# Small TensorE products spaced in the planner by instruction packets, and beta moved to one side of the delta rule

## The chip, the cores and the metric

The kernel runs on one core of one Trainium2 chip. The metric is the device time of one execution in microseconds (us). Three runs of the kernel before took 5138.00, 5150.58 and 5158.77 us; the median, 5150.58 us, is the time that counts.

## What is computed

There are 16 sequences of 512 tokens with 256 channels and 16 heads of 16 channels. Every one of them goes through three parts, of which only the first is touched.

```
q, k, v = x @ Wq + bq, x @ Wk + bk, x @ Wv + bv          # per head, 16 channels
k = k / (norm(k) + 1e-6);  beta = sigmoid(x @ Wbeta + bbeta)
S = S + beta_t * outer(v_t - S k_t, k_t);  o_t = S q_t      # the delta rule, one token after another
first = outputs @ Wo + bo                                    # gated delta net
second = causal attention over 16 heads, with RMS norm and rotary positions
third  = mixture of 16 experts, top 4, and a shared expert
```

Each of the blocks (delta net with experts, then attention with experts) is normalised before and added to its input.

## The kernel before, in words

The whole program is one list of stages, written by `stages()` (line 150 on). Each engine walks through the same list in its own function (`tensor`, `vector`, `scalar`, `gpsimd`, `sync`) and issues its own instructions of each stage, with semaphore waits between engines. So the list sets each engine's order of work, and an engine never goes past an instruction that waits. No stage is reordered at run time.

**The first stretch, delta net.** The tokens of one head are worked on in chunks of 16 tokens. One step of the list, m = 0 to 63, takes 128 rows: one chunk of each of 8 sequences; state is kept over the 32 steps of each half. For one m the stages are: `p_qk`, `p_v` (TensorE projections), `p_qk_out`, `p_v_out` (ScalarE copies, squares of k, and tanh for beta), `k_sum` (VectorE, L1387, sum of squares of 16 channels), `k_pow` (GpSimd, L1926 to L1944), `k_scale` and `k_turn` (VectorE, L1388 to L1409), `k_split` (ScalarE copies of k; on GpSimd L1950, which writes `keo`, keys parted by even and odd chunks), `d_pairs` (TensorE, L1073, products of the keys with keys and queries, two halves), `d_keep`, `d_send` and `d_fetch` (through HBM, so that the 16x16 triangles lie along the free axis), `d_row` (VectorE, 15 rows of forward substitution for two m at once, L1426 and L1429), `d_back` and `d_inverse` (through HBM again, L2055 and L2065), and then the recurrence: `s_read` (TensorE, L1087), `s_rest` (VectorE), `s_solve` (TensorE, L1098), `s_took` (ScalarE), `s_add` (TensorE, L1112), `s_new` (VectorE), and `d_out` (TensorE, L1123) with `s_rows`. Buffers of kqT, vT, k01, pairs and inv are a ring of NR = 7, so `p_qk` of m comes after `d_out` of m - 7; qk, vs, ks, beta and pw have two.

Before the change both v and k carry sqrt(beta): `k_pow` makes 1 + tanh (L1931), takes the square roots of the norm and of that number in one power of 32 elements (L1936), adds 1e-6 and multiplies by sqrt(0.5) (L1938, L1939), and scales v (L1942).

**Products of 32x32.** `d_pairs`, `s_read`, `s_solve`, `s_add` and `d_out` consist of 32x32 products in the four row and column strips of TensorE. In the trace each such product is two weight loads and two matmuls: 256 instructions for one `s_read`, `s_solve`, `s_add` or `d_out`, and 128 for one half of `d_pairs`.

**The planner.** Generators (strands) yield stages, and `turn_of` (L176) picks the next strand. `put` keeps a clock for each engine from the table TAKES (us for each stage and engine) and notes when a stage would be done; a strand may go on when TensorE's clock has reached its time `at`. The recurrence (`chain`) comes first in the list of strands, then `rows` (d_out), `relate` (d_pairs), `scale`, `project`, `solve`, `fetch`, `normalise` and `lift`, and behind these the experts' work: `heads`, `shares`, `sums` (gathers of expert output, y_ stages) and `tiles` (t_ stages). A rule holds `rows` and `relate` back for one turn if the latest TensorE stage was one of the five of FINE:

```
if latest[0] in FINE:
    able = [t for t in able if t not in fine] or able
```

`x_move` scatters rows to the experts by indirect DMAs of GpSimd (L2000), and `y_gather` fetches the experts' rows (L2009). A group of expert tiles can begin only after the rows of its four sequences are all scattered. The second stretch (attention, from about 2480 us) has a fixed order with a credit for tiles, and behind it the last tiles are worked off.

## Time and profile before

| what | value |
|---|---|
| median of 3 runs | 5150.58 us |
| the profiled execution, its own time | 5180.71 us |
| span of that profile | 5179.1 us |
| TensorE matmul busy | 3770.6 us (73%) |
| VectorE, ScalarE, GpSimd busy | 2499.1, 1987.3, 2069.6 us (48%, 38%, 40%) |
| mean granted clock of TensorE | 0.821 |
| instructions | 149179 |

The profile is one execution. The share of busy time is an average over stretches with different limits: the delta net takes the span up to about 2480 us, the attention up to about 4860 us, and the tail of expert tiles the rest. "issue" behind an idle time is time in which the engine waited for nothing that the profile shows.

### The profile page before, as it was taken

The page shows a single profiled execution, that of the slowest core. Times are in us where ns is not written, and L with a number is a line of the kernel's source. Part 1 is how long each engine was busy: PE and PEld are TensorE (multiplying, and loading weights), DVE is VectorE, ACT ScalarE, POOL GpSimd, SP SyncE. Part 2 cuts the span into 40 slices and gives each one's busy share as a digit, 9 for nine tenths or more (in the row PEclk, how much of TensorE's full clock was granted, in tenths as well). Part 3 has the DMA queues.
Part 4 walks back from the last instruction along what each step waited for, and adds up shares of the span by engine and source line. Part 5 has one row for each costly group of instructions (what it writes and reads, how often), then busy time and mean ns, then how long its engine had stood idle before and what let it go on. Part 6 is the DMA issues. An engine that isn't in the chain of part 4 may idle for free.

```text
span 5179.1 us, 149179 instructions
## 1 busy us (share of the span) xinstructions
PE 3770.6 (73%) x59789; PEld 2767.4 (53%) x59853; DVE 2499.1 (48%) x7106; ACT 1987.3 (38%) x4956; POOL 2069.6 (40%) x3064
## 2 busy tenths in 40 slices
PE   5666657786567865578658887688878887888776
PEld 3445435664346644357536664366655664566554
DVE  4343433324233344333447666676646763677243
ACT  2121112331013311113346665466546664666343
POOL 5332453115552245521373113731244326333554
PEclk7676667896569966668879998799989998899797
DMA  4222223552236623246534332243333443345565
GB/s 116 71 81 75 67 60 92 159 157 71 66 83 196 185 59 88 60 125 186 163 102 135 109 100 81 92 137 100 102 116 112 137 123 113 92 138 158 169 197 171
DMA packets 697353, 601.36 MB, mean 116 GB/s; under 512 B 337120, under 2 KB 576992, under 8 KB 696032
## 3 DMA queue, kind: packets, MB, share of 16 engines
q1 hardware_dynamic: 647520, 457.54, 31.5%
q0 software_dynamic: 49152, 134.28, 8.0%
q8 instruction: 483, 7.91, 0.7%
q14 instruction: 198, 1.62, 0.1%
HBM read 359.93 MB, written 231.60 MB: 114 GB/s over the span
## 4 chain that ended last, share of the span: by engine, by line
PE 24%; DVE 10%; issue 7%; ACT 5%; POOL 5%; DMA 1%; another core or an unknown queue 1%; SPq 0%; ACTq 0%; DVEq 0%; POOLq 0%
PE psum L1319 4%; PE psum L1166 3%; PE psum L1336 3%; POOL xbuck L2000 2%; DVE region L1536 2%; PE psum L1219 2%; PE psum L1188 2%; PE psum L1311 1%; PE psum L1301 1%; PE psum L1208 1%; PE psum L1240 1%; ACT region L1839 1%; POOL yg L2009 1%; PE psum L1176 1%
## 5 line engine op out<-in xcount | busy, mean ns | idle before, releaser
L2009 POOL DMA_INDIRECT yg<-ybuck,words x512 | 510.8, 998 | 653.9 <-DVE acc L1709 492.3
L1319 PE MATMUL psum<-xgT,w 128*128 128x128 f32 x4256 | 645.6, 300 | 124.9 <-issue 55.4
L1319 PEld LDWEIGHTS psum<-xgT,w 128*128 128x128 f32 x4256 | 581.2, 210 | 168.6 <-issue 129.4
L2000 POOL DMA_INDIRECT xbuck<-srow,words x512 | 511.0, 998 | 154.1 <-issue 141.3
L1536 DVE TENSOR_REDUCE region<-psum 128x1 f32<-128x384 f32 (+3 forms) x704 | 421.2, 635 | 162.8 <-PE psum L1191 132.6
L1981 POOL TENSOR_SCALAR_AFFINE_SELECT region<-region 128x128 f32<-128x128 f32 x1024 | 287.6, 301 | 494.5 <-ACT region L1839 483.2
L1839 ACT ACTIVATE region<-psum 128x512 f32<-128x512 f32 (+3 forms) x1024 | 390.5, 455 | 186.2 <-PE psum L1208 146.7
L1336 PE MATMUL psum<-w_w2T,hid 128*128 x1064 | 364.9, 427 | 93.1 <-DVE hid L1699 54.9
L1870 ACT ACTIVATE xgT<-psum 128x256 f32<-128x256 f32 x647 | 247.2, 382 | 378.3 <-PE psum L1301 301.0
L1936 POOL TENSOR_TENSOR region<-region 128x32 f32<-128x32 f32 x64 | 349.5, 5461 | 49.5 <-DVE region L1387 46.5
L1346 DVE SCALAR_TENSOR_TENSOR sil<-sil,psum 128x128 f32<-128x128 f32 (+1 forms) x419 | 123.9, 296 | 443.2 <-ACT sil L1885 325.4
L1073 PE MATMUL psum<-region 32*32 32x64 f32 x8192 | 204.8, 252 | 182.3 <-POOL region L1950 134.2
L1709 DVE SCALAR_TENSOR_TENSOR acc<-yg,words,acc 128x256 f32<-128x256 f32 x512 | 256.5, 501 | 154.8 <-DMA yg<-ybuck,words 67.8
L1693 DVE TENSOR_TENSOR hid<-sil,psum 128x128 f32<-128x128 f32 x268 | 76.7, 287 | 461.8 <-ACT sil L1883 330.1
L1188 PE MATMUL psum<-region 96*128 96x128 bf16 (+3 forms) x1024 | 258.3, 316 | 41.0 <-DVE region L1536 14.8
L1208 PE MATMUL psum<-region 128*128 128x384 bf16 (+3 forms) x960 | 247.2, 313 | 53.9 <-ACT region L1832 20.3
L1073 PEld LDWEIGHTS psum<-region 32*32 32x32 f32 x8192 | 167.5, 128 | 219.0 <-POOL region L1950 140.8
L1219 PE MATMUL psum<-region 128*32 128x512 f32 (+3 forms) x2048 | 225.6, 474 | 69.6 <-POOL region L1981 61.8
L1301 PE MATMUL psum<-w_ident,xg 128*128 128x128 f32 x1294 | 266.3, 291 | 13.3 <-DMA xg<-xbuck 9.6
L1891 ACT ACTIVATE yrow<-psum 128x256 f32<-128x256 f32 x647 | 249.0, 385 | 30.6 <-PE psum L1336 16.9
L1336 PEld LDWEIGHTS psum<-w_w2T,hid 128*128 128x128 f32 x1064 | 178.7, 205 | 133.6 <-issue 126.7
L1301 PEld LDWEIGHTS psum<-w_ident,xg 128*128 128x128 f32 x1294 | 193.6, 151 | 93.2 <-issue 21.5
(229 smaller groups left out, 7666.9 us busy)
## 6 DMA issues: line engine op xcount, KB each, us to landing
w<-in_w13T SPq DMA_DIRECT2D x532, 256.0 KB
xg<-xbuck SPq DMA_DIRECT2D x647, 128.0 KB
ybuck<-yrow SPq DMA_DIRECT2D x647, 128.0 KB
xbuck<-x SPq DMA_DIRECT2D x40, 512.0 KB, 3.9
pairs<-region SPq DMA_DIRECT2D x64, 256.0 KB
region<-pairs SPq DMA_DIRECT2D x512, 16.0 KB
inverse<-region SPq DMA_DIRECT2D x32, 256.0 KB
region<-inverse SPq DMA_DIRECT2D x512, 16.0 KB
```

The source lines that it names most:

```text
L1073: o = e.matmul(psum[p, mi, h % 8 * 64:h % 8 * 64 + 64], keo[p, h % 2, h // 2 * 32:h // 2 * 32 + 32], kqT[m % NR][p, :, h // 2, :], start=T ...
L1188: e.matmul(psum[:, mi, c:c + n], qT[0:96, h0 + i, qt * 128:n], kT[0:96, h0 + i, 0:n], start=(i == 0), stop=False, skip_group_check=True)
L1208: e.matmul(psum[:, mi, 0:n], kT[:, h, keys], qT[:, h, kt * 128:SEQ], start=True, stop=True, skip_group_check=True).then_inc(s["ws"], 1)
L1219: o = e.matmul(psum[32 * a:32 * a + 32, 6, kt * 128:SEQ], vb[:, kt, k % 4 * 4 + a, :], P[w % 16][:, 0:n], start=(kt == 0), stop=(kt == NQ ...
L1301: o = e.transpose(psum[:, mi, k * 128:(k + 1) * 128], xg[I % 5][:, k * 128:(k + 1) * 128], ident[:, :])
L1319: o = e.matmul(psum[:, mi, half], w13[I % 3][:, k, half], xgT[I % 2][:, k, :], start=(k == 0), stop=(k == 1), skip_group_check=True)
L1336: o = e.matmul(psum[:, mi, 0:D], hid[hi][:, 0:128] if f is None else hidT[f % 2], w2T[:, bass.ds(expert.pop(I), 1), :].rearrange("p a b -> ...
L1536: e.tensor_reduce(mx[:, qt, h0:h0 + nh], psum[:, mi, 0:nh * n].rearrange("p (h n) -> p h n", h=nh), AX.X, ALU.max).then_inc(s["mx"], 1)
L1839: e.activation(P[w % 16][:, 0:n], psum[:, mi, 0:n], ACT.Exp, scale=HD ** -0.5).then_inc(s["we"], 1)
L1936: e.tensor_tensor(flat, flat, half32, ALU.pow).then_inc(s["pw"], 1)
L2000: e.indirect_dma_start(xbuck[g % 2], bass.IndirectOffsetOnAxis(ap=posu[g % 2][:, J - ROWS0[g], k:k + 1], axis=0), srow[J % 2], None).then_ ...
L2009: e.indirect_dma_start(yg[y % 5], None, ybuck[g % 2][0:TILES_OF[g] * 128, :], bass.IndirectOffsetOnAxis(ap=posu[g % 2][:, j, k:k + 1], axi ...
```

## The change

There are two edits. **The planner:** the stages of 32x32 products are announced by their strand (`yield DENSE`), and such a strand is picked only once a modelled time `arrive` has come; each of the stages moves `arrive` on by FETCH = 3.6 us from the beginning of the one before the last. The rule on FINE is gone. `y_` stages are placed at TensorE's clock, and `sums` comes back after SUMS = 1.5 us of it. Four entries of TAKES are new, and `k_split` of m is put only after both halves of `d_pairs` of m - 1. **The delta rule:** beta (as 0.5 tanh + 0.5, on VectorE, L1387 before) multiplies v and one of the two copies of k; the other copy is k over its norm alone. GpSimd's power has 16 elements, and its two scalings are gone; VectorE has one product of 256 elements more and one of 16 less, and one transpose more (of the unit keys, from which GpSimd writes `keo`). The triangle is read by column in `d_row`. All waits on `kt` count four transposes for each m.

```diff
+DENSE = 0.36
 FINE = ("s_read", "s_solve", "s_add", "d_out", "d_pairs")
-HOP, SLACK, EVERY = 0.25, 0.6, 2.7
+HOP, SLACK, EVERY, SUMS, FETCH = 0.25, 0.6, 2.7, 1.5, 3.6
 LOADS = 3.2
 TAKES = {
     "ln_stat": [("DVE", 1.1)], "ln_rstd": [("POOL", 1.7)], "ln_norm": [("ACT", 1.2)], "ln_turn": [("PE", 0.5)],
     "ln_out": [("ACT", 0.6)], "p_in": [("SP", 0.5), ("DMA", LOADS)],
     "p_qk": [("PE", 2.1)], "p_qk_out": [("ACT", 1.0)], "p_v": [("PE", 1.2)], "p_v_out": [("ACT", 0.6)],
-    "k_sum": [("DVE", 0.45)], "k_pow": [("POOL", 7.2)], "k_scale": [("DVE", 0.9)],
-    "k_turn": [("DVE", 1.2)], "k_split": [("ACT", 1.0), ("POOL", 0.3)], "d_pairs": [("PE", 1.2)],
+    "k_sum": [("DVE", 0.6)], "k_pow": [("POOL", 4.0)], "k_scale": [("DVE", 1.1)],
+    "k_turn": [("DVE", 1.6)], "k_split": [("ACT", 1.0), ("POOL", 0.3)], "d_pairs": [("PE", 1.2)],
...
-        if stage[0].startswith("t_"):
+        if stage[0][:2] in ("t_", "y_"):
             moment[0] = free["PE"]
-        if TAKES.get(stage[0], [("", 0)])[0][0] == "PE":
-            latest[0] = stage[0]
+        if stage[0] in FINE:
+            begins.append(max(free["PE"], moment[0], arrive[0]))
+            arrive[0] = max(arrive[0], begins[-2]) + FETCH
...
-        if latest[0] in FINE:
-            able = [t for t in able if t not in fine] or able
-        t = able[0] if able else min(live, key=lambda t: t.at)
+        able = [t for t in able if not t.dense or now >= arrive[0]]
+        t = able[0] if able else min(live, key=lambda t: max(t.at, arrive[0]) if t.dense else t.at)
         if streams[1] in able and now - paced[0] > EVERY:
             t, paced[0] = streams[1], now
-        free["PE"] = max(now, t.at)
+        free["PE"] = max(now, t.at, arrive[0] if t.dense else 0.0)
         moment[0], n = t.at, len(order)
         hop[0] = HOP if t is strands[0] else SLACK
-        t.step()
+        t.dense = t.step() == DENSE
         if len(order) == n:
             t.at = free["PE"] + 0.2
         elif t is streams[1]:
             t.at = free["PE"]
+        elif t is streams[2]:
+            t.at = free["PE"] + SUMS
...
+            while m > 0 and m - 1 not in related:
+                yield LIGHT
             put("k_split", m)
             split.add(m)
...
+                yield DENSE
                 mi, mf = yield from misc.take()
                 put("d_pairs", m, half, mi, mf)
+                if half:
+                    related.add(m)
...
+            yield DENSE
             ai, af = yield from misc.take()
             put("s_read", m, ai, af)
             yield LIGHT
             put("s_rest", m, ai)
-            yield LIGHT
+            yield DENSE
...
             put("s_took", m, ui)
             misc.give(ui, "ue", m + 1)
-            yield LIGHT
+            yield DENSE
...
             m, ai = outs.popleft()
+            yield DENSE
             put("d_out", m, ai)
...
-                pe.wait_ge(s["kt"], 3 * m + 2)
+                pe.wait_ge(s["kt"], 4 * m + 3)
...
+                dv.wait_ge(s["pve"], m + 1)
+                e.tensor_scalar(beta[m % 2], beta[m % 2], 0.5, 0.5, ALU.mult, ALU.add).then_inc(s["n2"], 1)
+                e.tensor_reduce(pw[m % 2], sq.rearrange("p (h e) -> p h e", e=16), AX.X, ALU.add).then_inc(s["n2"], 1)
             elif name == "k_scale":
                 m, = u
-                f = pw[m % 2]
-                dv.wait_ge(s["pw"], 4 * m + 4)
-                e.reciprocal(f[:, 0, :], f[:, 0, :]).then_inc(s["kf"], 1)
+                f, k = pw[m % 2], qk[m % 2][:, 256:512].rearrange("p (h e) -> p h e", e=16)
+                unit = ks[m % 2].rearrange("p (h e) -> p h e", e=16)
+                dv.wait_ge(s["pw"], 2 * m + 2)
+                e.reciprocal(f, f).then_inc(s["kf"], 1)
                 dv.wait_ge(s["kf"], 3 * m + 1)
-                e.tensor_tensor(f[:, 0, :], f[:, 0, :], f[:, 1, :], ALU.mult).then_inc(s["kf"], 1)
-                dv.wait_ge(s["kf"], 3 * m + 2)
                 dv.wait_ge(s["pke"], m + 1)
                 dv.wait_ge(s["k01"], max(m - 1, 0))
-                e.tensor_tensor(ks[m % 2].rearrange("p (h e) -> p h e", e=16),
-                                qk[m % 2][:, 256:512].rearrange("p (h e) -> p h e", e=16), bc(f[:, 0, :], 2, 16),
-                                ALU.mult).then_inc(s["kf"], 1)
+                e.tensor_tensor(unit, k, bc(f, 2, 16), ALU.mult).then_inc(s["kf"], 1)
+                dv.wait_ge(s["kf"], 3 * m + 2)
+                dv.wait_ge(s["n2"], 2 * m + 1)
+                e.tensor_tensor(k, unit, bc(beta[m % 2], 2, 16), ALU.mult).then_inc(s["kf"], 1)
             elif name == "k_turn":
                 m, = u
                 if m >= NR:
                     dv.wait_ge(s["au"], m - NR + 1)
                 e.transpose(kqT[m % NR][:, 1, :, :].rearrange("p g t -> p (g t)"), qk[m % 2][:, 0:256]).then_inc(s["kt"], 1)
+                dv.wait_ge(s["kt"], 4 * m + 1)
+                e.transpose(qk[m % 2][:, 0:256], ks[m % 2]).then_inc(s["kt"], 1)
                 dv.wait_ge(s["kf"], 3 * m + 3)
-                e.transpose(kqT[m % NR][:, 0, :, :].rearrange("p g t -> p (g t)"), ks[m % 2]).then_inc(s["kt"], 1)
+                e.transpose(kqT[m % NR][:, 0, :, :].rearrange("p g t -> p (g t)"), qk[m % 2][:, 256:512]).then_inc(s["kt"], 1)
                 dv.wait_ge(s["vs"], m + 1)
                 e.transpose(vT[m % NR], vs[m % 2]).then_inc(s["kt"], 1)
...
-                e.tensor_tensor(tmp, bc(gram[n % 2][:, :, i, 0:i], 2, i), t[:, :, 0:i, 0:i], ALU.mult).then_inc(s["inv"], 1)
+                e.tensor_tensor(tmp, bc(gram[n % 2][:, :, 0:i, i], 2, i), t[:, :, 0:i, 0:i], ALU.mult).then_inc(s["inv"], 1)
...
-                    ac.wait_ge(s["kt"], 3 * m - 3)
+                    ac.wait_ge(s["kt"], 4 * m - 4)
+                    ac.wait_ge(s["keo"], m - 1)
...
-                ac.wait_ge(s["kf"], 3 * m + 3)
+                ac.wait_ge(s["kf"], 3 * m + 2)
...
-                po.wait_ge(s["pve"], m + 1)
-                po.wait_ge(s["kf"], max(3 * m - 3, 0))
-                e.tensor_scalar(f[:, 1, :], beta[m % 2], 1.0, 0.0, ALU.add, ALU.max).then_inc(s["pw"], 1)
-                po.wait_ge(s["pw"], 4 * m + 1)
-                po.wait_ge(s["n2"], m + 1)
+                f, v = pw[m % 2], vs[m % 2].rearrange("p (h e) -> p h e", e=16)
+                po.wait_ge(s["n2"], 2 * m + 2)
                 po.wait_ge(s["set"], 6)
-                flat = f.rearrange("p a h -> p (a h)")
-                e.tensor_tensor(flat, flat, half32, ALU.pow).then_inc(s["pw"], 1)
-                po.wait_ge(s["pw"], 4 * m + 2)
-                e.tensor_scalar(f[:, 0, :], f[:, 0, :], 1e-6, None, ALU.add).then_inc(s["pw"], 1)
-                e.tensor_scalar(f[:, 1, :], f[:, 1, :], math.sqrt(0.5), None, ALU.mult).then_inc(s["pw"], 1)
-                po.wait_ge(s["pw"], 4 * m + 4)
-                po.wait_ge(s["kt"], max(3 * m - 3, 0))
-                e.tensor_tensor(vs[m % 2].rearrange("p (h e) -> p h e", e=16),
-                                vs[m % 2].rearrange("p (h e) -> p h e", e=16), bc(f[:, 1, :], 2, 16),
-                                ALU.mult).then_inc(s["vs"], 1)
+                e.tensor_tensor(f, f, half, ALU.pow).then_inc(s["pw"], 1)
+                po.wait_ge(s["pw"], 2 * m + 1)
+                e.tensor_scalar(f, f, 1e-6, None, ALU.add).then_inc(s["pw"], 1)
+                po.wait_ge(s["kt"], max(4 * m - 4, 0))
+                e.tensor_tensor(v, v, bc(beta[m % 2], 2, 16), ALU.mult).then_inc(s["vs"], 1)
             elif name == "k_split":
                 m, = u
-                po.wait_ge(s["kt"], 3 * m + 2)
+                po.wait_ge(s["kt"], 4 * m + 2)
                 po.wait_ge(s["d_delta"], 48)
                 po.wait_ge(s["ga"], 2 * m)
-                e.tensor_tensor(keo, bc(kqT[m % NR][:, 0, :, :].rearrange("p g t -> p (g t)"), 1, 2), bc(par2, 2, 256),
-                                ALU.mult).then_inc(s["keo"], 1)
+                e.tensor_tensor(keo, bc(qk[m % 2][:, 0:256], 1, 2), bc(par2, 2, 256), ALU.mult).then_inc(s["keo"], 1)
```

## Rows read from the trace of the kernel before

**Rows 1.** Busy time by stretch: us, PE, PEld, DVE, ACT, POOL, granted clock, DMA share, GB/s

```profile
20.00:580.00 560.00, 370.07 (x12214) 266.75 (x12214) 231.36 (x731) 116.32 (x292) 212.11 (x226) 0.71 0.29 76
580.00:870.00 290.00, 174.85 (x5869) 125.60 (x5867) 103.23 (x319) 39.50 (x104) 149.76 (x149) 0.68 0.23 59
870.00:1150.00 280.00, 227.53 (x4140) 192.43 (x4138) 95.92 (x327) 101.93 (x311) 52.77 (x70) 0.90 0.62 168
1150.00:1540.00 390.00, 228.17 (x7147) 159.87 (x7151) 143.75 (x436) 52.91 (x140) 201.52 (x210) 0.66 0.27 71
1800.00:2260.00 460.00, 274.85 (x8869) 192.93 (x8856) 181.63 (x540) 62.33 (x165) 234.29 (x231) 0.67 0.27 71
4861.00:5180.00 319.00, 227.31 (x1033) 172.46 (x1031) 120.71 (x369) 124.33 (x446) 147.11 (x157) 0.87 0.58 176
```

**Rows 2.** Groups of TensorE's instructions, 0 to 2480 us: busy, mean ns | idle before, releasers

```profile
L1073 PE MATMUL psum<-region 32*32 32x64 f32 x8192 | 204.8, 252 | 182.3 <-POOL region L1950 134.2 <-issue 47.8
...
L1123 PE MATMUL psum<-region 32*32 32x32 f32 x8064 | 130.9, 223 | 100.6 <-issue 100.6
...
L1112 PE MATMUL psum<-region 32*32 32x32 f32 x7936 | 130.0, 223 | 94.8 <-issue 80.4 <-ACT region L1771 14.3
...
L1098 PE MATMUL psum<-region 32*32 32x16 f32 x8192 | 123.7, 191 | 153.2 <-issue 119.3 <-DVE region L1443 26.8 <-DVE region L1440 6.8
...
L1087 PE MATMUL psum<-region 32*32 32x32 f32 x8192 | 119.7, 210 | 57.6 <-issue 55.2 <-DVE region L1435 2.1
```

**Rows 3.** TensorE in order of time, around 510 us: start, us, what, [idle before]

```profile
509.66 1.14 PE L1098 MATMUL psum<-region 32*32 32x16 f32 x68 [0.97 <-issue]
...
511.29 1.06 PE L1112 MATMUL psum<-region 32*32 32x32 f32 x59 [0.49 <-ACT region L1771]
...
513.29 1.12 PE L1112 MATMUL psum<-region 32*32 32x32 f32 x67 [0.94 <-issue]
```

**Rows 4.** DMA queues, 333 to 389 us: the instruction queue (packets, MB, share of 16 engines)

```profile
q8 instruction: 11, 0.18, 1.3%
```

**Rows 5.** SyncE's queue in order of time: d_back of two pairs, one after the other

```profile
326.93 0.32 SPq L2055 DMA_DIRECT2D inverse<-region  x1
...
381.07 0.32 SPq L2055 DMA_DIRECT2D inverse<-region  x1
```

**Rows 6.** Line L1950 (keo): who waited for it, us and times

```profile
  PE psum L1073: 134.2, 24
```

**Rows 7.** Groups of GpSimd's instructions, 0 to 2480 us

```profile
L1936 POOL TENSOR_TENSOR region<-region 128x32 f32<-128x32 f32 x64 | 349.5, 5461 | 49.5 <-DVE region L1387 46.5
...
L1938 POOL TENSOR_SCALAR region<-region 128x16 f32<-128x16 f32 x64 | 16.8, 262 | 5.7
...
L1913 POOL TENSOR_TENSOR small<-small,halfpow 128x4 f32<-128x4 f32 x15 | 15.9, 1063 | 1.2
...
L2009 POOL DMA_INDIRECT yg<-ybuck,words x125 | 128.3, 1026 | 215.2 <-DVE acc L1709 193.3 <-issue 21.8 <-PE psum L1073 0.2
```

**Rows 8.** Line L1936 by stretch: us, busy (count), granted clock, DMA share, GB/s

```profile
580.00:870.00 290.00, 49.27 (x9) 0.68 0.23 59
1150.00:1540.00 390.00, 55.94 (x11) 0.66 0.27 71
1800.00:2260.00 460.00, 71.03 (x13) 0.67 0.27 71
```

**Rows 9.** Groups of VectorE's instructions, 0 to 2480 us

```profile
L1426 DVE TENSOR_TENSOR region<-region 128x2 f32<-128x2 f32 (+14 forms) x480 | 170.6, 355 | 8.4
...
L1398 DVE TENSOR_TENSOR region<-region 128x256 f32<-128x256 f32 x64 | 27.3, 426 | 2.2
...
L1407 DVE STREAM_TRANSPOSE region<-region 128x256 f32<-128x256 f32 x64 | 25.7, 402 | 0.0
...
L1394 DVE TENSOR_TENSOR region<-region 128x16 f32<-128x16 f32 x64 | 14.7, 230 | 2.2
```

**Rows 10.** Turns of expert tiles in the tail, 4861 to 5180 us (two for each tile)

```profile
L1301 PE MATMUL psum<-w_ident,xg 128*128 128x128 f32 x214 | 44.9, 297 | 3.1 <-DMA xg<-xbuck 3.1
```

More of the change, by code:

```diff
@@ L115, in __init__ @@
     def __init__(self, gen):
-        self.gen, self.done, self.result, self.credit, self.at = gen, False, None, 0.0, 0.0
+        self.gen, self.done, self.result, self.credit, self.at, self.dense = gen, False, None, 0.0, 0.0, False
     def step(self):
@@ L166, in put @@
         moment[0] += hop[0]
-    done, paced, latest = {}, [0.0], [""]
+    done, paced, arrive, begins = {}, [0.0], [0.0], [0.0, 0.0]
     def mark(*key):
@@ L243, in stages @@
     added, chained = {}, set()
-    blocks, split = deque(), set()
+    blocks, split, related = deque(), set(), set()
     def normalise():
@@ L933, in build @@
     qk, vs, ks = ([room([n]) for _ in range(2)] for n in (512, 256, 256))
-    beta, pw = [room([16]) for _ in range(2)], [room([2, 16]) for _ in range(2)]
+    beta, pw = ([room([16]) for _ in range(2)] for _ in range(2))
     sq, keo = room([256]), room([2, 256])
@@ L940, in build @@
     ueo, state = [room([544]) for _ in range(2)], room([16, 32])
-    half32, pieces = room([32]), room([520]).bitcast(BF)
+    half, pieces = room([16]), room([520]).bitcast(BF)
     left, middle, low = region[0:3, pairs_at:pairs_at + 1040], *(
@@ L1078, in tensor @@
                 pe.wait_ge(s["new"], m + 1)
-                pe.wait_ge(s["kt"], 3 * m + 2)
+                pe.wait_ge(s["kt"], 4 * m + 3)
                 pe.wait_ge(s[mf[0]], mf[1])
@@ L1386, in vector @@
                 dv.wait_ge(s["vs"], max(m - 1, 0))
-                e.tensor_reduce(pw[m % 2][:, 0, :], sq.rearrange("p (h e) -> p h e", e=16), AX.X, ALU.add).then_inc(s["n2"], 1)
+                dv.wait_ge(s["pve"], m + 1)
+                e.tensor_scalar(beta[m % 2], beta[m % 2], 0.5, 0.5, ALU.mult, ALU.add).then_inc(s["n2"], 1)
+                e.tensor_reduce(pw[m % 2], sq.rearrange("p (h e) -> p h e", e=16), AX.X, ALU.add).then_inc(s["n2"], 1)
             elif name == "k_scale":
                 m, = u
-                f = pw[m % 2]
-                dv.wait_ge(s["pw"], 4 * m + 4)
-                e.reciprocal(f[:, 0, :], f[:, 0, :]).then_inc(s["kf"], 1)
+                f, k = pw[m % 2], qk[m % 2][:, 256:512].rearrange("p (h e) -> p h e", e=16)
+                unit = ks[m % 2].rearrange("p (h e) -> p h e", e=16)
+                dv.wait_ge(s["pw"], 2 * m + 2)
+                e.reciprocal(f, f).then_inc(s["kf"], 1)
                 dv.wait_ge(s["kf"], 3 * m + 1)
-                e.tensor_tensor(f[:, 0, :], f[:, 0, :], f[:, 1, :], ALU.mult).then_inc(s["kf"], 1)
-                dv.wait_ge(s["kf"], 3 * m + 2)
                 dv.wait_ge(s["pke"], m + 1)
                 dv.wait_ge(s["k01"], max(m - 1, 0))
-                e.tensor_tensor(ks[m % 2].rearrange("p (h e) -> p h e", e=16),
-                                qk[m % 2][:, 256:512].rearrange("p (h e) -> p h e", e=16), bc(f[:, 0, :], 2, 16),
-                                ALU.mult).then_inc(s["kf"], 1)
+                e.tensor_tensor(unit, k, bc(f, 2, 16), ALU.mult).then_inc(s["kf"], 1)
+                dv.wait_ge(s["kf"], 3 * m + 2)
+                dv.wait_ge(s["n2"], 2 * m + 1)
+                e.tensor_tensor(k, unit, bc(beta[m % 2], 2, 16), ALU.mult).then_inc(s["kf"], 1)
             elif name == "k_turn":
@@ L1438, in vector @@
                 dv.wait_ge(s["sq"], m + 1)
-                dv.wait_ge(s["kt"], 3 * m + 3)
+                dv.wait_ge(s["kt"], 4 * m + 4)
                 e.tensor_tensor(rest, vT[m % NR], psum[:, mi, 0:256], ALU.subtract).then_inc(s["rest"], 1)
@@ L1738, in scalar @@
                 ac.wait_ge(s["pkm"], m + 1)
-                ac.wait_ge(s["n2"], m)
+                ac.wait_ge(s["n2"], 2 * m)
                 e.activation(sq, psum[:, mi, 256:512], ACT.Square).then_inc(s["psq"], 1)
                 if m >= 2:
-                    ac.wait_ge(s["kt"], 3 * m - 3)
+                    ac.wait_ge(s["kt"], 4 * m - 4)
+                    ac.wait_ge(s["keo"], m - 1)
                 e.activation(qk[m % 2], psum[:, mi, :], ACT.Copy).then_inc(s["pke"], 1)
@@ L1904, in gpsimd @@
                 e.memset(onesb, 1.0).then_inc(s["set"], 1)
-                e.memset(half32, 0.5).then_inc(s["set"], 1)
+                e.memset(half, 0.5).then_inc(s["set"], 1)
             elif name == "ln_rstd":
```

1 line of the change is left out of this document (removed).

## The prediction

> **What bounds the kernel now.** I read the busy time by stretch first [rows 1]. The delta net takes the span up to about 2480 us, and there no engine is full. While there are no expert tiles (20 to 870, 1150 to 1540 and 1800 to 2260 us) TensorE is busy 59% to 66%, VectorE 35% to 41%, GpSimd 38% to 52%, and TensorE's granted clock is 0.66 to 0.71. From 870 to 1150 us, with tiles to work on, TensorE is at 81% with a clock of 0.90. So the stretches without tiles are bound by the order of dependent stages, and TensorE idles in them: 115 + 162 + 185 = 462 us in the three that start at 580, 1150 and 1800 us.
>
> What ends this idle time is in the groups of TensorE's instructions [rows 2]. Two releasers stand out. The first is "issue" before the five groups of 32x32 products: 47.8 + 100.6 + 80.4 + 119.3 + 55.2 = 403.3 us. TensorE in order of time shows what it is [rows 3]: a group breaks off in its middle, waits, and goes on, and the restarts are 3.63 us apart. Between the two lie 68 and 59 matmuls with as many weight loads, 254 instructions. The instruction queue moved 11 packets of 0.18 MB together in 56 us [rows 4], 16 KB each, which is 256 instructions of 64 bytes. TensorE uses up a packet of such products in about 2 us (two runs of 1.1 us [rows 3]) and gets the next after 3.6. The second releaser is `keo`, L1950 on GpSimd, for which d_pairs waited 24 times, 134.2 us in all [rows 2, 6].
>
> **What can't be gained.** The pace of chunks is also held by the strand of the triangles: d_back of one pair of m comes at 326.93 and of the next at 381.07 us [rows 5], 54.1 us for a pair, 27.1 for one m. In it are 15 rows on VectorE and two trips through HBM, which the change leaves alone. Packets need less: 11 in 56 us at 3.6 us are 40 us [rows 3, 4]. So in the early stretch spacing fills gaps but does not set the pace.
>
> **Part 1, GpSimd's k_pow.** The power of 32 elements takes 5.461 us and one of 4 elements 1.063 [rows 7]. A straight line between them is 0.157 us for an element, so 16 elements take 1.063 + 12 x 0.157 = 2.95 us. The bounds are 1.06 and 5.46, and I take the line. That saves 2.51 us; L1938, whose place before k_scale goes, saves 0.26 (and the old 1 + tanh about as much ahead of it). GpSimd is 3.0 us lighter for each m. On the way to `keo` VectorE now has one product of 256 more (0.43), one of 16 less (0.23) and, before the sum, the scaling of beta (about 0.23) [rows 9]; the new transpose of the unit keys takes the place that the old one had. The way from k_sum to `keo` is so about 2.77 - 0.43 = 2.3 us shorter. At the least that counts at the 24 waits, 24 x 2.3 = 55 us; at the most for all 64 m with the whole 3.0 us, 192 us. The three stretches in which GpSimd also scatters rows hold 9 + 11 + 13 = 33 powers [rows 8], and there the planner's own clock of GpSimd (7.2 us for k_pow before, 4.0 now) holds the pace as well. I take 33 x 2.6 = **-86 us**, where 2.6 lies between 2.3 and 3.0.
>
> **Part 2, spacing.** No instruction is taken away. What can go is the 403.3 us in which TensorE stands in the middle of a group [rows 2], if projections, turns and output products are put there and later places shrink. Bounds are 0 and 403. From 870 to 1150 us little can be won, since TensorE is busy 81%; in the early stretch the triangles hold the pace [rows 1, 5]. And where no other work is ready, a planned gap replaces an unplanned one. I take a third, **-134 us**. Behind a stall that goes, the next late thing is VectorE's part of the same recurrence, for which L1098 already waited 26.8 us [rows 2].
>
> The Trainium skill speaks against this part: "Runtime: NRT & Kernel Launch", section "Instruction fetch mechanics", says that the refill in 16 KiB blocks is hidden because the sequencer issues instructions more slowly than they come. By that rule this term would be nothing and the sum 134 us smaller. The trace agrees with the block's size and not with the hiding.
>
> **Part 3, VectorE.** Each m brings one product of 256 (0.426), one transpose (0.402) and the small scaling of beta, and takes one product of 16 away (0.230) [rows 9]: +0.43 + 0.40 = 0.83 us, 53 us for 64 m. VectorE is busy 41% in the early stretch [rows 1], so I count about that share as path: **+22 us** (bounds 0 and 53). If its cover goes, it is all of 53, in the rows of the triangles. d_row reads the triangle by column instead of by row. The trace has no such pair to compare. Its 480 products take 170.6 us [rows 9]: bounds are 0 and another 170.6 if a strided operand halved the rate. The reductions of the same rows write with that stride already, so I take 0. `p_qk_out` now waits for `keo` of m - 2, two places back, and `k_sum` for `p_v_out`, which the list puts ahead of it: 0. If `keo` is late there, ScalarE stands, and behind it s_took and so s_add.
>
> **Part 4, what comes back.** Tiles are worked off in the delta net only while a group is ready, and some ran beside its stalls. If the third group finds a shorter rest of this stretch, tiles move to the tail, where 214 turns, so 107 tiles, took 319 us [rows 1, 10], 3.0 us each. I take 15 tiles, **+45 us** (bounds 0 and 40 tiles, 120 us). The spacing of `sums` (1.5 us) puts gathers closer; GpSimd already stood 193.3 us before them waiting for VectorE's sums [rows 7]. I count 0, and it is in the range.
>
> **The sum.** -86 - 134 + 22 + 45 = -153 us. The profiled execution took 5180.7 us, 30 us above the median of the three runs, and comes to 5028; the median of 5150.6 comes to 4998. I give **4998 us**.
>
> **Rivals.**
> *Everything is filled.* With all 403 us of stalls and all 134 of `keo` gone, less 22 and 100 given back, the time is 5150.6 - 415 = 4736; two thirds of that gain would be 4874. For it: the stretches with many stalls have much projection work, too. Against it: the pace of the triangles. Chance 0.12.
> *Only GpSimd's part counts.* The fetch is hidden anyway, or the gaps are only moved: -86 + 22 + 15 (5 tiles back) = -49, so 5102. Rows 2 show stalls, but not that they set the end. The skill's rule named above would give this case. Chance 0.15.
> *Nothing measurable.* The `keo` waits turn into waits for rows of the triangles, and the rest evens out: 5140. Chance 0.10.
> *Slower: the reservation is too wide.* Each half of d_pairs is only half a packet (128 instructions) but is given 3.6 us like the others. The plan so reserves 6 x 3.6 = 21.6 us for one m where 5 x 3.6 = 18 are needed. Stages of the recurrence then come 3.6 us later for each m, and the stalls that they replace give nothing. In 33 m [rows 8] that is +119 us; with -86 and +22 it is +55, so 5206 us. It decides if the pace of one m in the early stretch, 27.1 us now [rows 5], goes above 28. For it: 21.6 is already 80% of 27.1, so strands will queue. Against it: other work can go into the gap, which a stalled TensorE can't do. Chance 0.18.
>
> **How the numbers follow.** The forecast has 0.45. Faster by over 0.5% (26 us, about what a measurement of this kernel can tell from no change) are the forecast, the full gain and GpSimd alone: 0.45 + 0.12 + 0.15 = 0.72. Within 0.5% is 0.10, slower 0.18. The range: the forecast with its ends, a fuller k_pow and stalls by half (-192 - 200 + 22 + 70 = -300, so 4850), and up to 5170, which takes in GpSimd alone and no change and leaves out most of the slower case and the upper part of the full gain. The forecast's own range is 4900 to 5085.
>
> **What would show it.** L1936 should take 2.6 to 3.3 us. Waits for `keo` should fall from 134 to below 70 us, "issue" before the five groups from 403 to 200 to 300 us; the delta net, which now lasts to about 2480 us, should end by 2250 to 2330 us, with fewer tiles done before it. The mean of L1426 should stay at 355 ns. I am wrong if stalls vanish and the delta net is no shorter (gaps only planned), if they stay (the model of packets is off), or if GpSimd's idle time before y_gather grows well above 193 us and `keo` with it.

## The result

Five runs of the changed kernel took 5084.23 to 5112.67 us, median **5092.06 us**, against 5150.58 before (five runs, 5138.00 to 5158.77). The ratio is 0.9895 with a 95% interval of 0.9866 to 0.9924: faster, by 58 us. That is in the range and on the side that was forecast, but the sum had 153 us. On one of the chips of the experiments one run of the kernel before took 6472.33 us; it is left out of the ratios. The profiled execution took 5084.23 us (before 5180.71), so the two traces lie 96 us apart, more than the medians; 38 us of that are the spread of single executions.

Busy time by stretch of the changed kernel (columns and stretches as in [rows 1]):

```profile
20.00:580.00 560.00, 414.21 (x14185) 296.76 (x14186) 307.42 (x899) 129.49 (x330) 159.48 (x199) 0.74 0.31 80
580.00:870.00 290.00, 199.70 (x5681) 147.32 (x5681) 117.62 (x352) 58.36 (x165) 126.39 (x142) 0.72 0.37 98
870.00:1150.00 280.00, 213.74 (x4470) 177.02 (x4468) 102.10 (x345) 87.32 (x262) 52.68 (x74) 0.86 0.54 145
1150.00:1540.00 390.00, 234.29 (x5940) 174.75 (x5941) 159.51 (x450) 72.25 (x206) 176.62 (x197) 0.69 0.40 111
1800.00:2260.00 460.00, 288.81 (x7566) 220.66 (x7555) 186.02 (x556) 87.09 (x252) 182.22 (x206) 0.71 0.41 112
```

In the first 580 us TensorE does more work than before (414 against 370 us busy, 14185 matmuls against 12214). From 1150 to 1540 and from 1800 to 2260 us it is still busy only 60% and 63%, so those stretches stayed weak.

The groups of 32x32 products, which answer to [rows 2]:

```profile
L1083 PE MATMUL psum<-region 32*32 32x64 f32 x8192 | 196.4, 242 | 114.3 <-POOL region L1956 63.0 <-issue 50.7
...
L1108 PE MATMUL psum<-region 32*32 32x16 f32 x8192 | 139.6, 193 | 231.3 <-issue 141.4 <-DVE region L1457 47.7 <-DVE region L1454 38.2
...
L1133 PE MATMUL psum<-region 32*32 32x32 f32 x8192 | 122.0, 217 | 68.4 <-issue 66.9 <-ACT region L1786 1.1
...
L1122 PE MATMUL psum<-region 32*32 32x32 f32 x7936 | 121.8, 220 | 77.3 <-issue 63.0 <-ACT region L1786 13.8
...
L1097 PE MATMUL psum<-region 32*32 32x32 f32 x8192 | 112.9, 208 | 67.2 <-issue 58.0 <-DVE region L1462 5.6 <-DVE region L1449 3.3
```

"issue" before them is 50.7 + 141.4 + 66.9 + 63.0 + 58.0 = 380.0 us, where it was 403.3. The waits for `keo` (now L1956) fell from 134.2 to 63.0 us. VectorE now keeps s_solve waiting 85.9 us (L1457 and L1454), where it was 33.6.

GpSimd's groups (the power, `keo`, the gathers), which answer to [rows 7]:

```profile
L1946 POOL TENSOR_TENSOR region<-region 128x16 f32<-128x16 f32 x64 | 189.4, 2959 | 476.8 <-DVE region L1399 476.7
...
L1956 POOL TENSOR_TENSOR region<-region 128x512 f32<-128x512 f32 x64 | 66.8, 1043 | 382.6 <-PE psum L1083 294.9 <-DVE region L1419 87.4
...
L2014 POOL DMA_INDIRECT yg<-ybuck,words x165 | 164.4, 996 | 214.2 <-DMA ybuck<-yrow 96.7 <-DVE acc L1723 82.1 <-issue 35.2
```

The power takes 2.96 us (2.95 was worked out). But there are new waits: GpSimd stood 294.9 us before `keo` waiting for d_pairs (16.6 us before the change, in the row of L1950 below), and 96.7 us before gathers of rows that the tiles had not yet written.

VectorE's products of the triangle and the reciprocal that waits for the power, the first answering to [rows 9]:

```profile
L1440 DVE TENSOR_TENSOR region<-region 128x2 f32<-128x2 f32 (+14 forms) x480 | 210.5, 439 | 16.2 <-DMA region<-pairs 8.4
...
L1405 DVE RECIPROCAL region<-region 128x16 f32<-128x16 f32 x64 | 15.7, 245 | 91.4 <-POOL region L1948 91.2
```

The products by column take 0.439 us instead of 0.355, 40 us more in all. The reciprocal now waits 91.2 us for GpSimd. d_back of two pairs, which answers to [rows 5], is less evenly spaced:

```profile
309.79 0.32 SPq L2060 DMA_DIRECT2D inverse<-region  x1
...
370.01 0.32 SPq L2060 DMA_DIRECT2D inverse<-region  x1
```

This pair took 60.2 us; the steps beside it are 54.0 and 61.7 us, and the one after those 36.7. From the fourth to the tenth pair the first products lie 48.6 us apart in the mean, where it was 56.6.

### The profile page after: what moved, and what is told of

The parts are those of the page before. It is cut to its first block, busy times and chain, and to the rows that moved or that the text cites. A ratio compares the mean times of both kernels' runs of the same rounds, so it can differ in the third digit from the quotient of the medians.

```text
span 5083.0 us, 149255 instructions
## 1 busy us (share of the span) xinstructions
PE 3744.8 (74%) x59853; PEld 2738.2 (54%) x59853; DVE 2591.2 (51%) x7234; ACT 1983.2 (39%) x4956; POOL 1868.7 (37%) x2936
## 4 chain that ended last, share of the span: by engine, by line
PE 47%; issue 16%; DVE 15%; POOL 8%; ACT 6%; SPq 4%; DMA 3%; another core or an unknown queue 2%; DVEq 0%; ACTq 0%; POOLq 0%
PE psum L1329 7%; PE psum L1346 4%; PE psum L1072 3%; POOL xbuck L2005 3%; PE psum L1176 3%; PE psum L1108 3%; DVE region L1550 2%; SPq L2055 2%; PE psum L1122 2%; PE psum L1083 2%; PE psum L1133 2%; PE psum L1311 2%; PE psum L1229 2%; PE psum L1261 2%
## 5 line engine op out<-in xcount | busy, mean ns | idle before, releaser
L1946 POOL TENSOR_TENSOR region<-region 128x16 f32<-128x16 f32 x64 | 189.4, 2959 | 476.8 <-DVE region L1399 476.7
L1218 PE MATMUL psum<-region 128*128 128x512 bf16 (+3 forms) x1024 | 272.7, 321 | 53.2 <-ACT region L1847 20.0
L1108 PE MATMUL psum<-region 32*32 32x16 f32 x8192 | 139.6, 193 | 231.3 <-issue 141.4
L1108 PEld LDWEIGHTS psum<-region 32*32 32x32 f32 x8192 | 116.2, 123 | 258.1 <-issue 166.0
```

Of the source, the lines that this page charges most:

```text
L1108: o = e.matmul(psum[p, mi, h * 16:h * 16 + 16], inv[m % NR][p, h, :], restT[p, h * 16:h * 16 + 16], start=True, stop=True, skip_group_chec ...
L1218: e.matmul(psum[:, mi, 0:n], kT[:, h, keys], qT[:, h, kt * 128:SEQ], start=True, stop=True, skip_group_check=True).then_inc(s["ws"], 1)
```

## The experiments

All runs of experiments fell on chips on which the kernel before takes 4888 to 4902 us and not 5151, so every ratio here is to the kernel before on the same chip. Two readings of the traces are used through all of them. **Pauses inside groups** are all gaps over 0.1 us on TensorE before any but the first instruction pair of a group of 32x32 products, added up over the delta net. **The pace** is the number of d_row products that VectorE did from 200 to 580 us (15 for a pair of m), from the view of busy time by stretch for that one line.

### The new delta rule alone

```diff
 the planner, its table and its rule on FINE as before; only the instructions of the delta rule changed
```

> The new delta rule with the planner of before, its old rule and its old table. Theory A (the gain of the change, 58 us at the median, comes from GpSimd's lighter k_pow, and spacing gives about nothing): 40 to 90 us faster than before, 5060 to 5110 us, waits for keo about halved from 134 us. Theory B (the gain comes from spacing the groups): within 20 us of before, 5130 to 5170 us.

Measured: 4914.28 us, ratio 1.0049 (1.0032 to 1.0066), slower by 24 us. Theory B, too, had allowed no more than 20. The groups of d_pairs on TensorE, the power on GpSimd and the reciprocal on VectorE:

```profile
L1073 PE MATMUL psum<-region 32*32 32x64 f32 x8192 | 180.8, 253 | 157.7 <-POOL region L1946 144.8 <-issue 12.9
```

```profile
L1936 POOL TENSOR_TENSOR region<-region 128x16 f32<-128x16 f32 x64 | 190.8, 2981 | 382.4 <-DVE region L1389 382.2
```

```profile
L1395 DVE RECIPROCAL region<-region 128x16 f32<-128x16 f32 x64 | 15.4, 240 | 1.6 <-POOL region L1938 1.6
```

The power is 2.5 us shorter and the waits for `keo` are the same 144.8 us as in the trace of the kernel before on such a chip (144.3, below). Theory A has fallen. The reason stands in two rows of the kernel before that I had not weighed. VectorE's reciprocal, the first instruction behind k_pow:

```profile
L1392 DVE RECIPROCAL region<-region 128x16 f32<-128x16 f32 x64 | 15.6, 244 | 19.4 <-POOL region L1939 19.4
```

and `keo` on GpSimd:

```profile
L1950 POOL TENSOR_TENSOR region<-region 128x512 f32<-128x512 f32 x64 | 66.6, 1041 | 231.2 <-DVE region L1407 214.2 <-PE psum L1073 16.6
```

VectorE waited only 19.4 us for the power in the whole delta net (25.4 us on the chip of this experiment, and 1.6 us with the short power). `keo` waited 214.2 us for L1407, the transpose. So the transpose is late mostly because of its place in VectorE's order, and hardly because of the power. A shorter power only makes GpSimd wait longer there: 352.5 us for that transpose (L1409 of this kernel), against 187.4 in the kernel before on the same chip.

### The new planner alone

```diff
-"k_sum": [("DVE", 0.6)], "k_pow": [("POOL", 4.0)], "k_scale": [("DVE", 1.1)], "k_turn": [("DVE", 1.6)]
+"k_sum": [("DVE", 0.45)], "k_pow": [("POOL", 7.2)], "k_scale": [("DVE", 0.9)], "k_turn": [("DVE", 1.2)]
 and the instructions of the delta rule as before
```

> The delta rule of before with the new planner, its table kept at the old costs of k_sum, k_pow, k_scale and k_turn. Theory A: within 20 us of before, 5130 to 5170 us. Theory B: 5070 to 5120 us, with waits for keo still near 134 us.

Measured: 4778.41 us, ratio 0.9763 (0.9746 to 0.9780). The planner gives more than the whole gain, and more than theory B had (5070 to 5120 us against 5151 is 0.984 to 0.994). Waits for `keo` fell to 69.6 us with the long power in place, which no theory had expected.

### No gate on the groups

```diff
-SUMS, FETCH = 0.25, 0.6, 2.7, 1.5, 3.6
+SUMS, FETCH = 0.25, 0.6, 2.7, 1.5, 0.0
```

> The changed kernel with FETCH = 0, so that no group waits for its packet in the plan; the new table and the spacing of sums stay. Theory A: like the changed kernel, 5080 to 5110 us, and pauses inside groups no more than the 326 us of the changed kernel plus 40. Theory B: 5130 us or more, with pauses inside groups above 369 us.

Measured: 4919.94 us, ratio 1.0066 (1.0049 to 1.0083). The gate is what gains. Pauses inside groups are 217 us, though, not above 369 (that number was from the first chip). The waits for `keo` are 130.2 us, although k_split is held here, too, until d_pairs of m - 1 is placed:

```profile
  PE psum L1083: 130.2, 17
```

### The new placing of sums left out

```diff
-        if stage[0][:2] in ("t_", "y_"):
+        if stage[0].startswith("t_"):
...
-        elif t is streams[2]:
-            t.at = free["PE"] + SUMS
```

> The changed kernel with the y_ stages placed as before (own time, no SUMS). If closer gathers cost time by blocking GpSimd (it lost much of its early lead between 1000 and 2400 us), this is 20 to 60 us faster than the changed kernel, 5030 to 5070 us. If the spacing of the sums is what won tiles for the first stretch, it is 20 us or more slower. If neither, within 15 us of 5092.

Measured: 4780.34 us, ratio 0.9782 (0.9758 to 0.9806). Against the changed kernel (0.9832, 0.9811 to 0.9854, below) that is 0.5% faster, and the intervals don't overlap: the placing of sums costs about 25 us. The gathers on GpSimd, without it and then with it:

```profile
L2012 POOL DMA_INDIRECT yg<-ybuck,words x158 | 161.5, 1022 | 300.6 <-DVE acc L1721 183.2 <-issue 113.2 <-DMA ybuck<-yrow 3.8
```

```profile
L2014 POOL DMA_INDIRECT yg<-ybuck,words x169 | 169.5, 1003 | 187.9 <-DMA ybuck<-yrow 95.7 <-DVE acc L1723 56.7 <-issue 35.2
```

With it GpSimd stands 95.7 us before gathers whose rows are still being written; without it 3.8. Yet its whole idle time before gathers is the larger one without it (300.6 us), so this wait alone doesn't explain the 25 us.

### The changed kernel, and the kernel before, on such a chip

> The changed kernel as it is, on whatever chip these runs get, since the first batch ran on a chip where the kernel before took 4889 us and not 5151. Theory B (spacing is the gain, the new delta rule gives nothing by itself): ratio to before 0.975 to 0.985 where the chip is the fast one, 0.985 to 0.993 where it is the first. Theory A (the new delta rule adds to the spacing): ratio below 0.970 on the fast chip.

> The kernel before, for its trace on the same chip as the others. On the fast chip: span 4870 to 4900 us, pauses inside groups 230 to 260 us as in the run with the new delta rule alone, and waits for keo 130 to 150 us.

Measured: 4809.39 us, ratio 0.9832 (0.9811 to 0.9854); the kernel before in a single run 4886.20 us. Pauses inside groups are 232 us before and 181 after, and the waits for `keo` 144.3 and 89.3. TensorE's d_pairs and d_out in the kernel before:

```profile
L1073 PE MATMUL psum<-region 32*32 32x64 f32 x8192 | 176.0, 248 | 156.9 <-POOL region L1950 144.3 <-issue 12.6
...
L1123 PE MATMUL psum<-region 32*32 32x32 f32 x8192 | 128.5, 225 | 94.5 <-issue 94.5
```

The change gains 1.7% here and 1.1% on the first chip, and the intervals don't overlap. On the first chip the pauses inside groups are longer, 369 us before and 326 after, though the smallest distances of instruction packets are the same 3.3 to 3.5 us. What makes that chip different was not found.

From these runs the sum on such a chip is: new delta rule +24 us (1.0049), the other edits of the planner +8 (1.0066 against 1.0049, with intervals that overlap), the gate -114 (0.9832 against 1.0066), in all -82 us. The delta rule's price in the other setting, 0.9832 against 0.9763, is +34 us. That one holds the four new entries of the table, too; no run parts them.

### The triangle read by row

```diff
-                e.tensor_tensor(tmp, bc(gram[n % 2][:, :, 0:i, i], 2, i), t[:, :, 0:i, 0:i], ALU.mult)
+                e.tensor_tensor(tmp, bc(gram[n % 2][:, :, i, 0:i], 2, i), t[:, :, 0:i, 0:i], ALU.mult)
```

> The changed kernel with d_row reading the triangle by row, as before; this uses the coefficients on the wrong side of the diagonal, so the result of the delta net differs, and the work is the same. Theory: the column read took 40 us more of VectorE (480 products, 171 to 211 us) and most of it lies in the strand of the triangles: 15 to 40 us faster than the changed kernel. Rival: it is covered, within 8 us of it.

Measured: 4800.69 us, ratio 0.9816 (0.9794 to 0.9837), 9 us below the changed kernel with overlapping intervals, so not clear of nothing. VectorE's products, by row here and by column in the changed kernel on the same chip:

```profile
L1440 DVE TENSOR_TENSOR region<-region 128x2 f32<-128x2 f32 (+14 forms) x480 | 163.8, 341 | 19.3 <-DMA region<-pairs 11.5
```

```profile
L1440 DVE TENSOR_TENSOR region<-region 128x2 f32<-128x2 f32 (+14 forms) x480 | 212.5, 443 | 20.7 <-DMA region<-pairs 12.9
```

The program is otherwise the same, so 49 us of VectorE are the column read, and by the medians they are mostly covered. The 9 us don't account for the 24 to 34 us of the new delta rule, whose rest (a product and a transpose more) was only argued.

### Half a packet for half a d_pairs

```diff
-            arrive[0] = max(arrive[0], begins[-2]) + FETCH
+            arrive[0] = max(arrive[0], begins[-2]) + FETCH * (0.5 if stage[0] == "d_pairs" else 1.0)
```

> The changed kernel with each half of d_pairs counted as half a packet, 1.8 us. If the reservation was too wide (21.6 us for each m where 18 are needed), 20 to 60 us faster than the changed kernel. If the halves are not what the strands wait for, within 15 us of it. If small groups come together again, slower, with pauses inside groups up by 30 us or more.

Measured: 4904.30 us, ratio 1.0020 (1.0004 to 1.0035). This is the truer model of packets, and it loses the whole gain. Pauses inside groups are 195 us, only 14 more than in the changed kernel. So the reservation was not too wide, and pauses are not what the gate is worth: 14 us of them stand against 95 us of time. The waits for `keo`, 108.7 us against 89.3, are not enough either. The pace of the triangles goes with the time here. From 200 to 580 us, products of the triangle (us busy, count in brackets, granted clock, DMA share, GB/s): the kernel before, the new delta rule alone, no gate, half packets, and the changed kernel:

```profile
200.00:580.00 380.00, 35.41 (x99) 0.71 0.28 73
```

```profile
200.00:580.00 380.00, 42.15 (x96) 0.69 0.28 73
```

```profile
200.00:580.00 380.00, 40.91 (x90) 0.73 0.28 71
```

```profile
200.00:580.00 380.00, 41.38 (x93) 0.72 0.27 70
```

```profile
200.00:580.00 380.00, 52.36 (x118) 0.75 0.29 72
```

The three changed kernels that gain nothing did 96, 90 and 93 products (99 before), the changed kernel 118. The rows of a pair took 33 us in the kernel before, 27 in the changed kernel and 34 with half packets (mean of five pairs, first product to last reduction).

### The triangles' strand second in the list

This led to theory C: the gate helps because strands with small groups wait in the plan, and the strand `solve` then gets its turns. In the kernel before it is the sixth in a list of which the first that is able goes on, and it has one turn for each row.

```diff
-main = [Strand(chain()), *fine, Strand(scale()), Strand(project()), solving, Strand(fetch()), ...
+main = [Strand(chain()), solving, *fine, Strand(scale()), Strand(project()), Strand(fetch()), ...
 and k_split of m held until both halves of d_pairs of m - 1 are placed
```

> The kernel before, with the strand of the triangles (solve) second in the list of strands and k_split held until d_pairs of m - 1 is placed; no spacing by packets, old delta rule. Theory C (the gate on small groups gained time because the rows of the triangles came closer in VectorE's order, 33 us for 15 rows before and 27 after, and not because TensorE pauses less): rows in 20 to 28 us, a pair of m in less than 54 us, pauses inside groups still 210 to 250 us, and 30 to 110 us faster than before. Rival D (fewer pauses are the gain): within 20 us of before.

Measured: 4748.06 us, ratio 0.9711 (0.9693 to 0.9728), 140 us faster than before with no packet model at all, and more than the 110 us that theory C had at most. d_out and d_pairs on TensorE:

```profile
L1127 PE MATMUL psum<-region 32*32 32x32 f32 x8192 | 128.2, 222 | 95.4 <-issue 95.2
...
L1077 PE MATMUL psum<-region 32*32 32x64 f32 x8192 | 165.4, 233 | 48.8 <-issue 38.8 <-POOL region L1954 10.0
```

```profile
200.00:580.00 380.00, 36.26 (x112) 0.75 0.31 79
```

"issue" before d_out is 95.2 us where it was 94.5, and pauses inside groups rose from 232 to 269 us. Yet the kernel is faster than the changed one. So longer pauses can go with a shorter time; the time here isn't set by their sum. The pace is 112 products, a pair takes 50 us. The rows themselves took 30 us, not under 28; as much again lies in the time between one pair's last row and the next one's first, 20 us where it was 24.

And the waits for `keo` are 10.0 us, where they were 144.3. That leaves a rival to theory C: TensorE no longer waits for `keo`, 134 us less, which is near the 140 us of the gain. This run has two edits, `solve` ahead and k_split held back. The changed kernel without its gate parts them: with k_split held and `solve` in its old place the waits for `keo` are 130.2 us and nothing is gained, and with `solve` ahead as well (last experiment) they are 17.0. So it is the place of `solve` that ends these waits. Whether the time comes from them or from the rows of the triangles, no run shows, since none changes one without the other.

The delta net is 265 us shorter than before (last d_out starting at 2030 us against 2295), about twice the gain of the whole kernel. Only 158 expert tiles had been turned by then, where it was 218: the other 60 are done later.

### The best of the parts

```diff
 plan_no_sums: delta rule and its four entries of the table as before, new planner, sums placed as before
 plan_rows_first: the same, with the list of strands as in the diff above
```

> The delta rule of before with the new planner, without the new placing of the y_ stages. If the losses of the new delta rule (0.5% and 0.7% in two settings) and of the spacing of sums (0.5%) add up: ratio to before 0.970 to 0.974. If they don't, 0.976 or more.

> The same with the strand of the triangles second in the list of strands. Theory C with something left to win: ratio below 0.965. If the gate has taken all of it: within 15 us of the run without this.

Measured: 4745.51 us, ratio 0.9701 (0.9684 to 0.9719), and 4704.71 us, ratio 0.9628 (0.9610 to 0.9645). The first is what adding up the losses gives, and the second is the fastest of all, 184 us below the kernel before. Its pace:

```profile
200.00:580.00 380.00, 43.19 (x120) 0.79 0.30 76
```

### More waits in d_out

```diff
                 for x in range(4):
                     p = strips(x)
                     c = h // 2 * 32
+                    for _ in range(2):
+                        e.wait_ge(s["ue"], m + 1)
```

> The kernel before with 128 waits that are already met added to TensorE's program in each d_out: no matmul more, half a packet of 16 KB more for each m. If the pauses inside groups are the fetch of instructions: 32 packets more, pauses inside d_out and the groups behind it up by 50 to 115 us from 232 in all. If they are something else (a port, the clock, PSUM): unchanged within 20 us apart from the time that the waits themselves take.

Measured: 5256.14 us in a single run, 368 us slower. Of the 128 waits only 64 became instructions of their own (149179 instructions before, 153275 here), so 16 packets more and not 32. The rest of the question was overlaid by the price of a wait. The matmuls of d_out:

```profile
L1125 PE MATMUL psum<-region 32*32 32x32 f32 x8064 | 533.8, 226 | 26.5 <-issue 24.4
```

They span 533.8 us instead of 128.5. The row holds 63 of the 64 groups, so a group took 8.5 us instead of 2.0. And the pause before them is 24.4 us where it was 94.5. The forecast for a fetch (pauses up) failed as it was put. A group was now used up more slowly than packets come (8.5 us for one and a quarter packets, whose smallest distance is 3.3 us). That fits pauses that are a supply falling behind; it doesn't prove it.

### Is it the packet or the pace, in the changed kernel?

```diff
 after_rows_first:  the changed kernel with the list of strands as in rows_first
 fetch0_rows_first: the same with FETCH = 0.0
 fetch32, fetch44:  the changed kernel with FETCH = 3.2 and 4.4
```

> The changed kernel with the strand of the triangles second in the list of strands, nothing else. Theory C (the pace of the triangles' rows sets the delta net): 30 to 80 us faster than the changed kernel, ratio to before 0.967 to 0.977, a pair of m in under 49 us. If the gate has already taken this: within 15 us of the changed kernel, ratio 0.980 to 0.986.

> FETCH = 0 (no gate on small groups) with the strand of the triangles second. Without the gate alone the ratio was 1.0066 and a pair of m took 60 us. Theory C: the pace comes back with no gate, a pair in 54 us or less, ratio 0.975 to 0.990. If the gate itself is what counts (packets): ratio 0.998 or more.

> The changed kernel with FETCH = 3.2. If 3.6 counts as the true time of a packet, a plan with a slightly too short time is nearly as good: within 25 us of the changed kernel, ratio 0.979 to 0.988. If the gain hangs on the order that the gate happens to give, the ratio may be anywhere between that of the changed kernel and 1.007 (as with FETCH = 0).

> The changed kernel with FETCH = 4.4. If 3.6 is the true time of a packet: 10 to 60 us slower than the changed kernel, since 6 x 4.4 = 26.4 us for each m are reserved, more than the 25 us that an m takes. If spacing beyond the packet still helps the triangles' rows: not slower.

Measured: after_rows_first 4743.53 us, ratio 0.9681 (0.9665 to 0.9697). fetch0_rows_first 4774.88 us, 0.9749 (0.9732 to 0.9765). fetch32 4869.13 us, 0.9928 (0.9910 to 0.9945). fetch44 4798.38 us, 0.9797 (0.9767 to 0.9827).

Without the gate the kernel was 0.7% slower than before; without the gate and with `solve` second it is 2.5% faster. These two kernels differ in the place of `solve` alone, so this is the cleanest of the comparisons: 3.2% from one strand's place in the list. The waits for `keo` of the second, and its pace:

```profile
  PE psum L1083: 17.0, 5
```

```profile
200.00:580.00 380.00, 51.77 (x118) 0.76 0.30 73
```

118 products, as many as the changed kernel, with pauses inside groups of 268 us. So the early pace can be had with no gate. With `solve` second the gate adds 0.7% (0.9681 against 0.9749), where it added 2.3% without.

Two things did not go by theory C. A pair took 51.8 us in after_rows_first, not under 49, and the early pace was 111 products: its gain over the changed kernel comes after 580 us, since its last product of the triangle starts at 2042 us against 2205. And 3.6 us is no special value: 4.4 is no slower than 3.6, though it did only 105 products in the early stretch, and 3.2 loses more than half of the gain with 107. So the early pace does not rank these orders. The waits for `keo` in the whole delta net part them better: every kernel with 105.7 us or more of them gains at most 0.7% (3.2: 105.7, half packets: 108.7, no gate: 130.2, the new delta rule alone: 144.8), and every one with 89.3 us or less gains 1.7% or more (changed kernel: 89.3, 4.4: 56.5, after_rows_first: 19.8). That is a match and not a cause shown. What decides between such orders after 580 us, where GpSimd also scatters and gathers, stays open.

## Why the prediction was right and wrong

**What bounds the kernel: right, as far as the runs show.** The delta net is bound by the order of dependent stages: moving one strand in the list shortened the kernel by 3.2%. That the triangles hold the early pace fits most runs and was not shown apart from the waits for `keo`. I used that only to cut the gain from pauses, and not to ask what the gate would do to this strand.

**Part 1, k_pow, -86 us: wrong.** 2.95 us for 16 elements was right (2.96). The step that failed is "at the least that counts at the 24 waits". It put the 134.2 us of waits for `keo` [rows 6] down to the power. The two rows quoted above show that VectorE waited for the power 19.4 us and `keo` 214.2 us for VectorE. The new delta rule alone left the waits for `keo` at 144.8 us (144.3 before) and cost 24 us, where Parts 1 and 3 together had a gain of 64. The lower bound should have been 0, and what a shorter power can free for VectorE in that order about 19 us.

**Part 3, VectorE, +22 us: about right.** Parts 1 and 3 together cost 24 us (34 in the other setting); with Part 1 at nothing that is the forecast with its bounds. I took 0 for the column read; it was 40 to 49 us of VectorE, of which some 9 us reached the time by the medians, with intervals that overlap. That the reductions write with the same stride said nothing of reading. The Trainium skill has this rule ("SBUF — State Buffer", "Door 1: The DMA port swizzle"): accesses stay at full rate within 16-byte lines, and each that crosses to a new line pays. The trace agrees: a stride of 16 float32 elements is 64 bytes, and the products took 0.439 us instead of 0.355.

**Part 2, spacing, -134 us: the size was near by luck, the mechanism wrong.** The gate gave -114 us on the fast chip. But with the gate pauses were only 36 us less there (217 and 181; the whole change took off 51, and "issue" fell by 23 on the first chip, where 100 to 200 were forecast), and a kernel with longer pauses than before was faster still. The step that failed is that the time of the stalls that go is time won. What changed is whose turn it is in the plan: rows of the triangles were placed closer, and d_pairs waited less for `keo`. The Trainium skill ("Runtime: NRT & Kernel Launch", "Instruction fetch mechanics") calls the fetch mostly hidden. If the pauses of 181 to 369 us in these traces are the fetch, as the distances of packets suggest, they say otherwise. Its consequence for the time, that the fetch does not set the end, fits the runs better than my mechanism, though the -114 us of the gate lie nearer to my figure.

**Part 4, +45 us: wrong.** No tiles went to the tail. Before the last d_out 237 tiles had been turned, where it was 218, with the delta net 59 us shorter (last d_out starting at 2425 us against 2484, first chip). What this part describes did come where `solve` was moved ahead: 60 tiles fewer in the delta net, and about half of its 265 us given back. And I had counted the placing of sums at 0; it costs 25 us on the fast chip.

**The signs to look for.** L1936 at 2.6 to 3.3 us (2.96) and waits for `keo` below 70 us (63.0) came true. "issue" at 200 to 300 us (380.0), the end of the delta net at 2250 to 2330 us (2425) and an unchanged L1426 (0.439) did not.

**The rivals.** The reservation was not too wide: halving it for d_pairs lost all, and 4.4 us was no worse. Only GpSimd's part counts: it is the one part that does not. Everything is filled: 380.0 us of stalls are left. Nothing measurable: the gain is clear of the noise.

**The size on the first chip.** Part 1 missing (86 us) and the sums (25), less the 45 that did not come back, make 153 into 87, against 82 on the fast chip; with Part 2 right in size by luck, this sum is no proof of its parts. The 58 us of the first chip are less, and that difference is not explained.

## What to carry to other kernels

Before a shorter operation is priced, look at how long its next consumer waited for it; a long wait further down the chain may have been released by something else's place in an in-order queue. In a kernel whose order comes from a planner, an edit of one cost or rule acts on whose turn it is, so test it against a plain change of priority: here that gave 2.9% (with k_split held back), where the packet model with its new delta rule gave 1.7%. A truer model is not a better plan by itself, and small changes of its constants moved the time by 1% to 2%. A first stretch that ends earlier is not all gain where other work had filled its gaps: 265 us there were 140 in the whole.

## What the hardware showed that I had not expected

A product on VectorE of 128x450 elements in float32 took 677 ns in the mean with its broadcast operand read along the row, and 924 with a stride of 16 elements. The same shape of that line in the kernel before and with the new delta rule alone:

```profile
L1426 DVE TENSOR_TENSOR region<-region 128x450 f32<-128x450 f32 x32 | 21.7, 677 | 0.7
```

```profile
L1430 DVE TENSOR_TENSOR region<-region 128x450 f32<-128x450 f32 x32 | 29.6, 924 | 0.7
```

With two waits, long met, written before each of the 64 products of d_out, a group took 8.5 us instead of 2.0, and the kernel 368 us more (a single run; 64 of the 128 waits of a group became instructions of their own).
